# First maxima in ones and twos between the quarters of a feature product, and the last group's query blocks in the order second, third, fourth, first

## The chip, the cores and the metric

The kernel runs on one core of a Trainium2 chip. The metric is the device time of one execution in microseconds (us), the median of several runs. TensorE (PE) multiplies matrices into eight PSUM banks, VectorE (DVE) and ScalarE (ACT) work on PSUM and SBUF, GpSimd (POOL) on SBUF alone. SyncE (SP), ScalarE and GpSimd issue DMA transfers. The engines run on their own and wait for each other's semaphores.

## The reference

The input x is 2 x 2048 x 512. One transformer layer is computed in float32: causal attention with grouped keys, a layer norm, a soft mixture of experts, and a second layer norm. The change touches the attention alone:

```python
q = (x @ Wq).reshape(b, n, NUM_KV_GROUPS, GROUP_SIZE, HEAD_DIM)   # 4 groups of 4 heads, 32 wide
k = (x @ Wk).reshape(b, n, NUM_KV_GROUPS, HEAD_DIM)
v = (x @ Wv).reshape(b, n, NUM_KV_GROUPS, HEAD_DIM)
scores = jnp.einsum('bqgsd,bkgd->bgsqk', q, k) * scale
scores = jnp.where(causal, -jnp.inf, scores)
attn = jax.nn.softmax(scores, axis=-1)
ctx = jnp.einsum('bgsqk,bkgd->bqgsd', attn, v)
...
x = _layernorm(x + (ctx.reshape(b, n, D_OUT) @ Wo + bo), axis=-1)
```

## The kernel before

Five stages run one after the other, each ended by a barrier of all engines: `projections` (to 191.6 us), `attention` (to 1167.9 us), `post`, `slots` and `combine`.

**projections** works through eight blocks of 512 tokens (`NBLK`). For a block, TensorE transposes the input into the four banks of `ps_t`, and makes six features (`m` 0 to 3 queries of a group, 4 keys, `VT` = 5 values) into the four banks of `ps_f`. A feature is a sum over four quarters `c` of the 512 inputs, and each quarter takes three products (`three_passes`, L73 to L75), since every operand is split into a high and a low half. ScalarE reads a finished feature as its high half (`features_hi`, L320), VectorE makes the low half (`features_lo`, L356), and SyncE's `store` writes both to DRAM. SyncE's `first_loads` brings the first group's operands back into SBUF.

The softmax needs the largest score of each row ahead of the scores. One **unit** `u` is one product of 128 queries of a head with up to 512 keys; its rows' maxima are read by VectorE (`maximum`): by `tensor_reduce` where all keys are allowed, and by a masked form where the unit touches the diagonal. A unit's number of columns is 128, 256, 384 or 512. `MAXU` lists the units by query block. Those of the first two query blocks (`AHEAD` = 2), 48 units, are done inside projections, when `ps_t` has no more inputs to transpose: `units_behind(blk, m)` spreads them over ten places, each behind a whole feature, four or five at a place. Unit `u` takes bank `u % 4` of `ps_t` and waits until unit `u - 4` is read. VectorE takes a place's units right behind that feature's low half. After a query block's last unit, `maximum_rows` folds the maxima into rows (`s_max`), and SyncE copies each block's rows into `q` with four small transfers, at the very end of its work (L190).

**attention** has eight groups (`ITERS`: two batches, four key groups), each with four query blocks of 512 (`QB`). A query block `qb` has 4 * qb + 4 steps of 128 keys, so the first is short (4 steps) and the fourth long (16). A step has four **scores** (one per head, L1060), four exponentials on ScalarE (L1142) and a **context** product (L1078). The last four steps of a block lie on the diagonal: they are narrower (512, 384, 256, 128 columns), and GpSimd's `select` (L961) clears the upper triangle ahead of the context product. The sums of a row's exponentials are made partly on GpSimd, by `add` of whole steps (L981) and by transfers that add one step onto another (`move`, L994), partly on TensorE (`late_sums` L1089 for steps left over, `block_sums` L1098 for GpSimd's sum). VectorE turns them (`flip`, `inverse`), GpSimd multiplies (`normalise`, L1003), SyncE stores. The short block has no adds. A block's scores wait for its row transfers (`s_row`). A block's queries are loaded over those of the group before (`queries`, L889), as soon as the scores that read them are done.

The order of all this is written ahead by `plan()`: a greedy planner with modelled times chooses TensorE's next piece among scores, maxima (up to 80 units ahead of the scores, `M_LEAD`) and packed products. Every engine's program follows the list `order()`. `BLOCKS` gives the order of the query blocks: in each group 0, 1, 2, 3.

## Time and profile before

| | us |
|---|---|
| median of 3 runs (2526.11 to 2528.24) | 2528.2 |
| the profiled execution | 2528.26 |
| its span, first to last instruction | 2526.5 |
| attention's first product | 191.6 |
| last group's first score | 1033.9 |
| last exponential of attention | 1147.9 |
| post begins | 1167.9 |

The page gives for the span of 2526.5 us: TensorE busy 2413.8 us (96%), VectorE 1737.0, ScalarE 1426.1, GpSimd 1610.2. Busy times are averages over stages with different bounds; what counts at a place is which wait ends last there. All times below are us from the span's start.

### The profile page before, as it was taken

To read this page: it belongs to the slowest core of one execution; us is meant where nothing else is said; L and a number is where in the kernel's file an instruction comes from. 1 tells how busy PE (TensorE), PEld (TensorE's weight loads), DVE (VectorE), ACT (ScalarE), POOL (GpSimd) and SP (SyncE) were. 2 spreads that over 40 slices of the span, in tenths; PEclk is the share of its full clock that TensorE was granted. 3 is DMA by queue.
4 is the path that set the end of the run, shared out by engine and by line. 5 is a ranking of instruction groups with operands and counts; after the bars stand their busy time and mean duration, and the time that the engine had idled before them with its cause. 6 is when DMAs were issued, how large, how long until landed. Compare 5 with 4: busy or idle time off the path is not lost. (4 is left out here: it accounts for less than half of the span.)

```text
span 2526.5 us, 38828 instructions
## 1 busy us (share of the span) xinstructions
PE 2413.8 (96%) x12834; PEld 1726.7 (68%) x12834; DVE 1737.0 (69%) x3804; ACT 1426.1 (56%) x2761; POOL 1610.2 (64%) x1751
## 2 busy tenths in 40 slices
PE   8979999999999999996979999999999997999998
PEld 6865555555555555544767888887888885788886
DVE  3358778888888888833876655666656564877776
ACT  3215556666666666663865555666656554454553
POOL 4404577777877767776957667675576765555554
PEclk9999899999999999998989999999999998999999
DMA  7853655574656566555964545466445457674553
GB/s 248 270 169 84 132 124 125 115 151 113 145 112 145 118 144 123 116 107 157 355 202 138 166 137 159 145 217 186 152 141 160 132 164 245 189 226 131 148 151 102
DMA packets 249177, 400.87 MB, mean 159 GB/s; under 512 B 57712, under 2 KB 112016, under 8 KB 237584
## 3 DMA queue, kind: packets, MB, share of 16 engines
q1 hardware_dynamic: 196000, 283.48, 36.8%
q0 software_dynamic: 52480, 114.37, 20.5%
q8 instruction: 102, 1.67, 0.3%
q14 instruction: 99, 0.81, 0.1%
q10 hardware_dynamic: 496, 0.54, 0.1%
HBM read 180.63 MB, written 112.22 MB: 116 GB/s over the span
## 5 line engine op out<-in xcount | busy, mean ns | idle before, releaser
L1142 ACT ACTIVATE p_probs<-p_ps_s 128x512 f32<-128x512 f32 (+3 forms) x1280 | 591.1, 541 | 327.0 <-PE p_ps_s L1060 310.1
L1727 POOL DMA_DIRECT2D p_eT<-p_ex x1024 | 538.4, 535 | 272.9 <-DVE p_ex L1993 220.4
L1169 DVE TENSOR_REDUCE p_parts<-p_ps_m 128x1 f32<-128x512 f32 x752 | 459.1, 681 | 82.9 <-PE p_ps_m L1045 74.6
L1060 PE MATMUL p_ps_s<-q,k_e 98*128 98x512 f32 (+3 forms) x1280 | 468.4, 387 | 3.5 <-ACT p_probs L1142 3.1
L1045 PE MATMUL p_ps_m<-k_m,q 96*128 96x512 f32 (+2 forms) x1232 | 434.6, 387 | 11.9 <-PEq L2268 10.2
L981 POOL TENSOR_TENSOR p_added<-p_added,p_probs 128x2048 f32<-128x2048 f32 x88 | 419.4, 4769 | 34.5 <-ACT p_probs L1142 17.0
L1060 PEld LDWEIGHTS p_ps_s<-q,k_e 98*128 98x128 f32 x1280 | 241.8, 191 | 183.6 <-ACT p_probs L1142 76.3
L1078 PE MATMUL p_ps_c<-p_probs,v_e 128*32 128x512 f32 (+3 forms) x2560 | 285.3, 547 | 10.0 <-POOL p_probs L961 10.0
L1045 PEld LDWEIGHTS p_ps_m<-k_m,q 96*128 96x128 f32 x1232 | 235.4, 194 | 86.4 <-DVE p_parts L1173 20.2
L2127 POOL TENSOR_TENSOR p_acc<-p_acc,logit 128x512 f32<-128x512 f32 x112 | 162.5, 1451 | 153.6 <-ACT logit L2180 150.1
L1173 DVE CUSTOM_DVE_ANT_0 p_masked<-p_ps_m,p_mask 128x128 f32<-128x128 f32 (+1 forms) x480 | 203.9, 485 | 25.7 <-PE p_ps_m L1045 25.6
L73 PE MATMUL p_ps_l<-kept_hi,w_o_lo 128*128 128x512 f32 x512 | 208.0, 406 | 7.1 <-DVE w_o_lo L1940 6.4
L73 PE MATMUL p_ps_s<-xl_hi,w_o_hi 128*128 128x512 f32 x512 | 205.6, 402 | 8.8 <-DVE w_o_hi L1987 8.8
L74 PE MATMUL p_ps_s<-xl_lo,w_o_hi 128*128 128x512 f32 x512 | 204.7, 400 | 0.0
L75 PE MATMUL p_ps_s<-xl_hi,w_o_hi 128*128 128x512 f32 x512 | 204.7, 400 | 0.0
L1847 ACT ACTIVATE logit<-p_ps_l,kept_inv 128x512 f32<-128x512 f32 x128 | 87.8, 687 | 203.0 <-PE p_ps_l L75 203.0
L75 PE MATMUL p_ps_l<-kept_hi,w_o_lo 128*128 128x512 f32 x512 | 201.7, 394 | 0.0
L74 PE MATMUL p_ps_l<-kept_xT,w_o_lo 128*128 128x512 f32 x512 | 201.0, 393 | 0.0
L2180 ACT ACTIVATE logit<-logit 128x512 f32<-128x512 f32 x128 | 80.7, 631 | 150.4 <-DVE logit L2213 150.3
L1078 PEld LDWEIGHTS p_ps_c<-p_probs,v_e 128*32 128x32 f32 x2560 | 65.3, 110 | 126.1 <-issue 63.8
L1956 DVE TENSOR_REDUCE p_col<-logit 128x1 f32<-128x512 f32 x128 | 87.5, 684 | 85.3 <-ACT logit L1847 85.3
L1998 DVE TENSOR_TENSOR p_siT_lo<-p_ps_e,p_siT_hi 128x512 fp32r<-128x512 f32 x32 | 22.1, 692 | 159.3 <-ACT p_siT_hi L1882 159.3
(204 smaller groups left out, 4979.4 us busy)
## 6 DMA issues: line engine op xcount, KB each, us to landing
p_probs<-p_probs POOLq DMA_DIRECT2D x56, 1024.0 KB, 7.9
logits_t<-logit SPq DMA_DIRECT2D x32, 1024.0 KB, 5.0
p_eT<-p_ex POOLq DMA_DIRECT2D x1024, 32.0 KB, 2.1
logit<-logits_t SPq DMA_DIRECT2D x128, 256.0 KB, 3.5
q<-q_t SPq DMA_DIRECT2D x96, 256.0 KB, 4.8
c_first<-L_ffn_W_dram SPq DMA_DIRECT2D x64, 256.0 KB, 5.6
p_probs<-p_probs POOLq DMA_DIRECT2D x16, 768.0 KB, 7.5
p_x<-L_attn_x_dram SPq DMA_DIRECT2D x32, 256.0 KB, 4.7
```

Of the source, the lines that this page charges most:

```text
L73: pe.matmul(out, w_hi, m_hi, start=start, stop=False)
L74: pe.matmul(out, w_hi, m_lo, start=False, stop=False)
L75: return pe.matmul(out, w_lo, m_hi, start=False, stop=stop)
L981: pool.tensor_tensor(a[:, :, :], first[:, :, :], probs[s % RING][:, :, :], ALU.add).then_inc(s_add, 1)
L1045: pe.matmul(ps_m[:, bank("maximum", u), 0:w], q[0:QROWS, qb, h, bass.ts(t, P)], k_m[:, c * BLK:c * BLK + w], start=True, stop=True).then_i ...
L1060: pe.matmul(ps_s[:, u % ST_BANKS, q0:BLK], k_e[:, bass.ts(kt, P)], q[:, qb, h, q0:BLK], start=True, stop=True).then_inc(s_score, 1)
L1078: mm = pe.matmul(ps_c[part, 0, q0:BLK], v_e[:, kt, :], probs[s % RING][:, h, q0:BLK], start=s == FIRST[n], stop=last)
L1142: act.activation(probs[s % RING][:, h, q0:BLK], ps_s[:, u % ST_BANKS, q0:BLK], ACT.Exp).then_inc(s_exp, 1)
L1169: dve.tensor_reduce(to, bank, AX.X, ALU.max).then_inc(s_taken, 1)
L1173: dve.tensor_tensor_reduce(masked[u % 3][:, 0:w], bank, mask[:, BLK - w:], 1.0, -3.0e38, ALU.add, ALU.max, to).then_inc(s_taken, 1)
L1727: pool.dma_start(eT[r][p * QD:(p + 1) * QD, i, :, :], ex[i * QD:(i + 1) * QD, 2 * r:2 * r + 2, bass.ts(p, P)]).then_inc(s_eT[r], 16)
L2127: pool.tensor_tensor(a[:, :], a[:, :], lg[n % U][:, :], ALU.add).then_inc(s_acc, 1)
```

## The change

It has four parts. (1) The first 48 units get 36 places: behind each quarter `c` of the products of features 2 to 5 of block 6 and 0 to 4 of block 7, one unit or two. VectorE takes a feature's units ahead of that feature's low half. The value feature of the last block has no units. (2) `send_rows(0)` moves into SyncE's store of the last block, ahead of feature 2; `send_rows(1)` goes to ScalarE, behind its last copy. (3) In the last group, the query blocks come in the order 1, 2, 3, 0; `PREV` and `NEXT` name a block's counterpart in the neighbouring groups, and waits on key and value parts stand at every first use of a part. (4) VectorE waits for its mask at the first masked unit instead of at attention's start.

```diff
-        places = [(NBLK - 2, m) for m in range(2, VT + 1)] + [(NBLK - 1, m) for m in range(VT + 1)]
+        places = [(NBLK - 2, m, c) for m in range(2, VT + 1) for c in range(DC)] + [(NBLK - 1, m, c) for m in range(VT) for c in range(DC)]
-        def units_behind(blk, m):
+        def units_behind(blk, m, c):
...
+        def send_rows(eng, n):
+            eng.wait_ge(s_max, n + 1)
+            for a in range(4):
+                to = first[0][QROWS:MROWS, n, :, :].rearrange("o h (t a j) -> o h t a j", t=4, a=4)[:, :, :, a, :]
+                eng.dma_start(to.bitcast(F32), rows[n][a * 32:(a + 1) * 32, :]).then_inc(s_row[n], 16)
@@ sync: store
                 for m in range(NF):
+                    if blk == NBLK - 1 and m == 2:
+                        send_rows(sp, 0)
@@ sync: end
-            for n in range(AHEAD):
-                sp.wait_ge(s_max, n + 1)
...
@@ tensor: features
                         last = three_passes(pe, ps_f[:, bank(blk, m), :], w_hi[:, c, w], w_lo[:, c, w],
                                             xT_hi[j][:, c, :], xT_lo[j][:, c, :], c == 0, c == DC - 1)
+                        for u in units_behind(blk, m, c) if c < DC - 1 else []:
+                            unit(u)
                     last.then_inc(s_f, 1)
-                    for u in units_behind(blk, m):
+                    for u in units_behind(blk, m, DC - 1):
                         unit(u)
@@ scalar: end
+            for n in range(1, AHEAD):
+                send_rows(act, n)
@@ vector: features_lo
                 for m in ms:
+                    for c in range(DC):
+                        for u in units_behind(blk, m, c):
+                            maximum(u)
                     dve.wait_ge(s_fhi, blk * NF + (m + 1))
...
-                    for u in units_behind(blk, m):
-                        maximum(u)
@@
-BLOCKS = [(n // QB, n % QB) for n in range(NBK)]
+BLOCKS = [(it, qb) for it in range(ITERS) for qb in (range(QB) if it + 1 < ITERS else (1, 2, 3, 0))]
+SAME = {(it, qb): n for n, (it, qb) in enumerate(BLOCKS)}
+PREV = [SAME.get((it - 1, qb)) for it, qb in BLOCKS]
+NEXT = [SAME.get((it + 1, qb)) for it, qb in BLOCKS]
@@ attention, sync: queries
-                sp.wait_ge(s_score, 4 * END[n - QB])
+                sp.wait_ge(s_score, 4 * END[PREV[n]])
@@ attention, tensor: unit, scores, context
-                    if c == qb:
-                        pe.wait_ge(s_km[c], 48 * it)
+                    pe.wait_ge(s_km[c], 48 * it)
...
+                if it > 0 and kt % 4 == 0 and h == 0:
+                    pe.wait_ge(s_ke[kt // 4], 48 * it)
...
+                if it > 0 and kt % 4 == 0:
+                    pe.wait_ge(s_v[kt // 4], 16 * it)
@@ attention, vector
+                    if u == FIRST_MASKED:
+                        dve.wait_ge(s_mask, 1)
...
-            dve.wait_ge(s_mask, 1)
```

TensorE in projections, block 6, feature 2 (`p_ps_f` is the feature's bank, `p_ps_t<-k_m,q` a unit). Before:

```order
L73 MATMUL p_ps_f<-p_xT_hi,p_w_hi 128x512
L74 MATMUL p_ps_f<-p_xT_lo,p_w_hi 128x512
L75 MATMUL p_ps_f<-p_xT_hi,p_w_lo 128x512
L282 MATMUL p_ps_t<-k_m,q 128x128 x4
L73 MATMUL p_ps_f<-p_xT_hi,p_w_hi 128x512
```

and after, the feature's first two quarters and what follows the third:

```order
L73 MATMUL p_ps_f<-p_xT_hi,p_w_hi 128x512
L74 MATMUL p_ps_f<-p_xT_lo,p_w_hi 128x512
L75 MATMUL p_ps_f<-p_xT_hi,p_w_lo 128x512
L288 MATMUL p_ps_t<-k_m,q 128x128
L73 MATMUL p_ps_f<-p_xT_hi,p_w_hi 128x512
L74 MATMUL p_ps_f<-p_xT_lo,p_w_hi 128x512
L75 MATMUL p_ps_f<-p_xT_hi,p_w_lo 128x512
L288 MATMUL p_ps_t<-k_m,q 128x128
...
L288 MATMUL p_ps_t<-k_m,q 128x128 x2
```

The four units that stood behind the feature's last quarter now stand one, one, two behind its first three quarters.

SyncE at the end of projections: the last block's stores, the values' store and the row transfers. Before:

```order
L155 DMA q_t<-p_f_lo 128x512
L155 DMA k_t<-p_f_hi 128x512
L155 DMA k_t<-p_f_lo 128x512
L157 DMA v<-p_v 128x4x128
L190 DMA q<-first_rows 2x16x32 x8
```

and after, from the store of feature 1:

```order
L164 DMA q_t<-p_f_lo 128x512
L145 DMA q<-first_rows 2x16x32 x4
L164 DMA q_t<-p_f_hi 128x512
...
L164 DMA k_t<-p_f_lo 128x512
L166 DMA v<-p_v 128x4x128
```

Four row transfers now stand ahead of six stores, and the values' store is SyncE's last; the other four follow ScalarE's last copy (L333).

GpSimd at attention's end (`p_added` an add, `p_out` the product of normalise). Before:

```order
L981 TENSOR_TENSOR p_added<-p_added,p_probs 128x2048
L961 AFFINE_SELECT p_probs<-p_probs 128x4x128 x3
L981 TENSOR_TENSOR p_added<-p_added,p_probs 128x2048 x2
L1003 TENSOR_TENSOR p_out<-p_raw,p_inv 128x512
```

and after:

```order
L995 TENSOR_TENSOR p_added<-p_added,p_probs 128x2048
L975 AFFINE_SELECT p_probs<-p_probs 128x4x128 x3
L995 TENSOR_TENSOR p_added<-p_added,p_probs 128x2048
L975 AFFINE_SELECT p_probs<-p_probs 128x4x128 x2
L995 TENSOR_TENSOR p_added<-p_added,p_probs 128x2048
L975 AFFINE_SELECT p_probs<-p_probs 128x4x128 x2
L1017 TENSOR_TENSOR p_out<-p_raw,p_inv 128x512 x2
```

Two of the short block's selects stand ahead of the long block's last add, two behind it, and two products end the stage instead of one. On TensorE, the long block's first score is score 1217 of 1280 before and 1201 after, and the short block's 16 scores are the last. In groups one to seven no instruction of attention changes its place.

## Rows read from the trace of the kernel before

**Rows 1.** The page, part 2: granted TensorE clock in 40 slices of 63.2 us, tenths.

```profile
PEclk9999899999999999998989999999999998999999
```

**Rows 2.** Busy time of stretches: stretch, length, each engine's us, clock, DMA share, GB/s.

```profile
134.90:181.40 46.50, 39.43 (x178) 30.76 (x176) 30.58 (x93) 6.93 (x12) 0.00 (x0) 1.00 0.60 178
181.40:191.60 10.20, 0.03 (x1) 0.01 (x1) 2.81 (x12) 0.00 (x0) 0.02 (x1) 0.64 0.12 31
191.60:198.10 6.50, 6.48 (x16) 5.31 (x17) 4.98 (x8) 3.40 (x7) 1.54 (x5) 0.51 0.48 163
```

**Rows 3.** Waits from 140 to 192 us: waiter and releaser, us in total, times, longest.

```profile
PE p_ps_t L282 <- DVE p_parts L380: 4.7, 4, 1.3
...
PE p_ps_t L282 <- DVE p_parts L374: 2.2, 2, 1.2
```

**Rows 4.** TensorE's timeline: start, length, instruction, count, and the idle time before it.

```profile
179.49 1.50 PE L282 MATMUL p_ps_t<-k_m,q 96*128 96x384 f32 x5
...
191.62 0.77 PE L1045 MATMUL p_ps_m<-k_m,q 96*128 96x512 f32 x1 [10.19 <-PEq L2268]
```

**Rows 5.** VectorE's timeline: five unmasked maxima, and the last copy of the values.

```profile
156.68 3.07 DVE L374 TENSOR_REDUCE p_parts<-p_ps_t 128x1 f32<-128x512 f32 x5
...
183.67 0.65 DVE L366 COPY p_v<-p_ps_f 128x512 f32<-128x512 f32 x1
```

**Rows 6.** SyncE's queue: the values of block 6, the last key store, the row transfers.

```profile
165.03 0.37 SPq L157 DMA_DIRECT2D v<-p_v  x1
...
177.08 0.64 SPq L155 DMA_DIRECT2D k_t<-p_f_lo  x1
...
184.76 5.37 SPq L190 DMA_DIRECT2D q<-first_rows  x8
```

**Rows 7.** ScalarE's timeline: the last copy of projections, the last exponentials of attention.

```profile
179.69 0.60 ACT L327 ACTIVATE p_vT<-p_ps_f 128x512 f32<-128x512 f32 x1 [4.35 <-PE p_ps_f L75]
...
1146.63 1.25 ACT L1142 ACTIVATE p_probs<-p_ps_s 128x256 f32<-128x256 f32 x5 [1.51 <-PE p_ps_s L1060]
```

**Rows 8.** Busy time of three stretches of the last group.

```profile
1033.70:1094.20 60.50, 60.50 (x440) 34.49 (x441) 49.79 (x124) 39.11 (x85) 41.20 (x25) 1.00 0.40 88
1094.20:1147.90 53.70, 48.35 (x259) 18.75 (x257) 6.62 (x22) 36.82 (x82) 44.48 (x20) 0.94 0.58 118
1147.90:1167.90 20.00, 7.25 (x64) 2.33 (x64) 2.60 (x5) 0.60 (x1) 13.72 (x7) 0.73 0.04 14
```

**Rows 9.** TensorE's timeline: the long block's first scores, its product of sums.

```profile
1102.26 0.97 PE L1060 MATMUL p_ps_s<-q,k_e 98*128 98x512 f32 x3 [0.21 <-DMA q<-p_rows]
...
1160.65 1.94 PE L1098 MATMUL p_ps_m<-p_added,p_ones 128*32 128x512 f32 x8 [5.07 <-POOL p_added L981]
```

**Rows 10.** GpSimd's timeline at attention's end.

```profile
1149.27 2.10 POOL L961 TENSOR_SCALAR_AFFINE_SELECT p_probs<-p_probs 128x512 f32<-128x512 f32 x3
1151.05 9.46 POOL L981 TENSOR_TENSOR p_added<-p_added,p_probs 128x2048 f32<-128x2048 f32 x2
1164.76 1.26 POOL L1003 TENSOR_TENSOR p_out<-p_raw,p_inv 128x512 f32<-128x512 f32 x1 [4.26 <-issue]
```

**Rows 11.** TensorE's timeline, the short block: narrow scores, two contexts, late sums.

```profile
1044.12 0.33 PE L1060 MATMUL p_ps_s<-q,k_e 98*128 98x128 f32 x2
...
1047.36 1.28 PE L1078 MATMUL p_ps_c<-p_probs,v_e 128*32 128x384 f32 x16
...
1050.54 2.36 PE L1089 MATMUL p_ps_m<-p_probs,p_ones 128*32 128x512 f32 x32
```

**Rows 12.** The query loads of line 889: time from issue to landing.

```profile
DMA to landing us min/median/max: 3.8/4.8/8.1
```

**Rows 13.** Stretches of the first group, columns as before, and TensorE's timeline there.

```profile
266.00:270.00 4.00, 2.48 (x13) 0.59 (x16) 1.05 (x8) 0.28 (x1) 3.42 (x5) 0.52 0.00 0
282.00:286.00 4.00, 3.96 (x17) 2.50 (x13) 3.74 (x14) 0.92 (x2) 3.08 (x1) 0.84 0.00 0
...
267.66 3.21 PE L1078 MATMUL p_ps_c<-p_probs,v_e 128*32 128x512 f32 x16 [1.52 <-POOL p_probs L961]
```

More of the change, by code:

```diff
@@ L185, in _ @@
                 store(blk)
-            for n in range(AHEAD):
-                sp.wait_ge(s_max, n + 1)
-                for a in range(4):
-                    to = first[0][QROWS:MROWS, n, :, :].rearrange("o h (t a j) -> o h t a j", t=4, a=4)[:, :, :, a, :]
-                    sp.dma_start(to.bitcast(F32), rows[n][a * 32:(a + 1) * 32, :]).then_inc(s_row[n], 16)
         @block.gpsimd
@@ L406, in _ @@
                 features_lo(blk, range(2, NF))
-                for u in units_behind(blk, VT):
-                    maximum(u)
+                for c in range(DC):
+                    for u in units_behind(blk, VT, c):
+                        maximum(u)
             values(NBLK - 1)
@@ L434 @@
 U0 = M_END[AHEAD - 1]
+FIRST_MASKED = min(u for u in range(U0, NU) if MAXU[u][1] == BLOCKS[MAXU[u][0]][1])
 ADDED = [[], [0, 1, 3], [0, 1, 2, 3, 5, 6, 7], [0, 2, 4, 6, 7, 9, 11]]
@@ L538, in maximum_ready @@
         n = MAXU[u][0]
[L539 removed]
+        if PREV[n] is not None and 4 * END[PREV[n]] - 1 not in self.scored:
             return INF
[L541 removed]
+        return max(self.bank_free(), self.scored[4 * END[PREV[n]] - 1] + 6000 if PREV[n] is not None else 0)
     def ring_free(self, s):
@@ L672, in scores @@
             self.jobs.append((lambda: self.move_ready(s), "move", s))
-        if s == END[n] - 1 and n + QB < NBK:
-            self.moves.append((self.scored[u], "queries", n + QB))
+        if s == END[n] - 1 and NEXT[n] is not None:
+            self.moves.append((self.scored[u], "queries", NEXT[n]))
         if qb == QB - 1 and it + 1 < ITERS and s - FIRST[n] in (3, 7, 11, 15):
```

10 lines of the change are left out of this document (2 added, 8 removed).

## Prediction

> **What bounds the kernel now.** I read the granted clock by slices first, then the busy time of stretches, then the timelines of the two places that the change touches. TensorE's clock is at nine tenths or more in 36 of 40 slices [rows 1]; slice 5 (253 to 316 us) and slice 19 (1137 to 1200 us) hold two of the four dips, and the second lies at attention's end. The change touches the last 47 us of the first stage with the hand-over to attention, and the last 134 us of attention. All else, post, slots and combine (from 1167.9 us), keeps its instructions, so it should move as a block.
>
> First place. From 134.9 to 181.4 us TensorE is busy 39.4 of 46.5 us while VectorE works 30.6 us [rows 2]. The waits are TensorE's for VectorE: 6.9 us in six waits of up to 1.3 us, each at the fifth first maximum behind a feature, whose bank of ps_t is not yet read [rows 3]. Then TensorE stands still for 10.2 us: the last five maxima start at 179.49, and attention's first product at 191.62 [rows 4]. What fills the gap: VectorE reads maxima until 183.7 and copies the values at 183.67 to 184.32 [rows 5]; SyncE then issues the values' store and eight row transfers in 5.37 us, until 190.13 [rows 6]; the barrier takes 1.5 us more. The stage ends with SyncE's queue.
>
> Second place. Until 1094.2 us TensorE is busy all 60.5 of 60.5 us: TensorE bound. From there to 1147.9, with no maxima left, it is busy 48.4 of 53.7, and in the 20.0 us after the last exponential 7.3 [rows 8]. In those 20 us GpSimd sets the pace: three selects, two adds of together 9.46 us to 1160.5, then the block's product of sums, flip, inverse and the output's product at 1164.76 [rows 9, 10].
>
> **The change, part by part.**
>
> *Maxima one by one.* The same 48 units go behind 36 quarters, one or two each, instead of four or five behind ten features. Products added: none; removed: none. What goes is the 6.9 us. Is VectorE fast enough? A feature costs TensorE 12 products at 0.228 us (2.74 us) and 5.3 units at up to 0.235 us (1.25), 3.98 us. VectorE needs 5.3 x 0.61 us (five in 3.07 [rows 5]) plus the low half at 0.61, 3.88 us. That is nearly even where units are 512 wide (u 10 to 31), looser elsewhere. With four banks between them I keep 0.7 us of waits. Ends: 0, and 6.9 if the wait returns at other places. On the other side the last five units (1.1 us) now lie ahead of the value feature, no longer behind it. The value feature so ends at 179.5 - 6.9 + 0.7 + 1.1 = 174.4.
>
> *What follows it.* After the value feature no maxima are queued on VectorE, only the values: ScalarE's copy 0.2 us behind the feature, 0.60 us long [rows 7], the transposes, VectorE's copy 0.65: done 2.3 us after the feature, at 176.7; before it was 4.8 us.
>
> *Row transfers.* Eight at 0.67 us each [rows 6] were SyncE's last work. Now four stand in SyncE's store of the last block, four on ScalarE behind its last copy. ScalarE: 174.4 + 0.8 + 4 x 0.67 = 177.9. It delays nothing there, since ScalarE has no more work in the stage; its price on ScalarE's queue isn't in the trace, ends 1.2 to 4 us in all. SyncE's queue has to be followed too, for all is queued behind it: from the store of block six's values at 165.03 to the last key store's end, 177.72, it issues 21 transfers in 12.7 us [rows 6]. That start depends on VectorE's copy of those values, which comes 3.5 us sooner (the three waits ahead of it, 3.5, less four more units, 0.9, and a copy no longer queued behind four maxima, about 0.9). So 161.5 + 12.7 + 2.7 = 176.9, then the values' store at 177.3. ScalarE ends last at 177.9, SyncE 0.6 us before. Barrier 1.4: attention starts at 179.3 instead of 191.6. **Gain 12.3 us**, ends 8 and 14.5.
>
> *The mask wait* moves from VectorE's start of attention to its first masked unit. VectorE's first unit was released within 0.2 us of it: nothing.
>
> *The clock at the hand-over.* It fell 3 us into the idle time and came back 6.4 us after attention began; the stretch 191.6 to 198.1 ran at 0.51 [rows 2]. The idle time shrinks from 10.2 to some 4 us, and a wait of only 1.52 us, near 266 us, lies in a stretch at 0.52 [rows 13]. So I expect it to fall still, and come back a little sooner: 0.5 us, ends 0 and 3.
>
> *Order of the last group.* Up to the group's start nothing moves. The short block (16 scores, 4 contexts, 4 late sums) goes from first to last. While TensorE is the bound, its work is time: scores at 0.11 to 0.24 us each (two narrow ones in 0.33), 2.6 us; contexts 2.7 (the middle two 1.28); late sums 2.36 [rows 11]; 7.7 us. Also the third block's last, narrow scores stood alone before, after the last maximum, and waited for ScalarE: about 1.8 us, which go since maxima now stand between them. The long block so starts 9.5 us sooner than 1102.26 [rows 9] counted from the group's start. Ends 7 and 11.
>
> Does something hold it back? The long block's queries are now wanted twenty scores sooner. Their load starts with the group, has three transfers and takes 3.8 to 8.1 us each, median 4.8 [rows 12]; TensorE reaches the first unit that needs them some 6 us after the group starts. Wait 0.2 us, ends 0 and 3.3. The long block's row transfers get as much work ahead of its first score as before: no wait.
>
> *The tail.* T is the last exponential of the long block; before, attention ended at T + 20.0. The long block's run (45.6 us) and GpSimd's work in it stay. Now: add done T + 1.4, three selects to T + 3.2, add to T + 7.8, the short block's first two selects (1.25) to T + 9.1, add to T + 13.7, two selects to T + 15.0 [rows 10]. Beside these, ScalarE's 16 exponentials end by T + 11 (the last five took 1.25 [rows 7]). Then on TensorE the block sums (1.0 at full clock, 1.94 before [rows 9]) to T + 15.3, contexts 0.9, late sums 2.4 [rows 11] to T + 19.0; flip, reciprocal, transpose 2.0; product 1.3; to the next stage 1.9: T + 24.3. That is 4.3 us longer, ends 0 and 8. **Gain 9.5 - 4.3 - 0.2 = 5.0 us.**
>
> **Sum.** 12.3 + 0.5 + 5.0 = 17.8 us. The profiled execution took 2528.26 us (span 2526.5 and 1.8 around it), the median is 2528.2. So 2528.3 - 17.8 = **2510.4 us**. With the ends of the large terms halved against each other, 2506 to 2515.
>
> A rule speaks against the one-by-one form. In the trace the 6.9 us of short waits left the clock at 1.00 until 181 us, but the wait of 1.52 us before 267.66 us lies in a stretch at 0.52, and the clock was not back until the stretch 282 to 286 us [rows 2, 13]. The Trainium skill, page "TensorE: Matmul & The Clock Gate", section "A second HAM failure mode: psum-queue depth-cycling", says that small pauses between groups of products that cycle through PSUM banks make the clock swing between its levels. By that rule the 36 places could do this, and the sum would lose 8 us and more (rivals three and four); by the rows alone it loses nothing.
>
> **The rivals.**
>
> *One, VectorE sets the pace* in the first stage. 3.88 against 3.98 us per feature is close, and the low half now waits behind its feature's units. If 4 us of waits come back, the value feature ends at 178 and attention starts at 183: 2514 us. For it: the even pace. Against it: VectorE's whole work there, 30.6 us, is 9 less than TensorE's [rows 2].
>
> *Two, the tail eats the gain.* The short block's contexts and sums stand in TensorE's queue behind the long block's product of sums, which waits for GpSimd's last add, and GpSimd takes two selects ahead of that add. If the tail is T + 28 and the long block gains 7: minus 1 instead of plus 5, 2516 us.
>
> *Three, a clock spell.* One at half clock as after 266 us: the shifted start meets a pause at another moment. Some sixteen us at half clock [rows 13] cost up to 8 us: 2518. The same spell could vanish instead, which would give 2503.
>
> *Four, slower than before.* Each of the 36 places makes TensorE wait for VectorE's read, and the clock stays at 1.2 GHz for the stretch of 39 us of work. Price 39 us at most, 2549 us. It decides from the point where more than about 18 us are lost, 0.5 us a place or 18 us of work at half clock in that stretch; slower by over 0.2% from 23 us. Against it: the clock's row stays at 1.00 through waits of 1.3 us there.
>
> **How the numbers follow.** Forecast 0.72; one 0.12; two 0.08; three 0.05; four 0.03. A measurement tells about 0.2% (5 us) from no change. The first four cases are faster by more, less a 0.02 for several misses at once; that 0.02 is within; four is slower: faster 0.95, same 0.02, slower 0.03. The range from 2504 to 2518 takes in the forecast's ends, case one, two and most of three.
>
> **What the profile after would show.** Attention's first product at 179.3 (177 to 183), TensorE's waits for maxima in the first stage under 1.5 us, ScalarE's row transfers ending last before the barrier. The long block's first score near 1080.5, its last exponential near 1126, post's start near 1150. The forecast is wrong if the waits in the first stage stay above 3 us, if SyncE ends over 1 us after ScalarE, if the long block's first score is less than 7 us closer to the group's start, or if the tail behind its last exponential is over 28 us.

## The result and the profile after

The changed kernel took 2503.6 us, the median of four runs (2497.7 to 2505.7), against 2527.15 before (2525.9 to 2528.2). The ratio is 0.9903, with an interval from 0.9888 to 0.9919: 24 us, or 1%, faster. The forecast of 2510.4 was wrong: the gain is larger than the 17.8 us forecast, and the median lies 0.4 us under the range. The profiled execution is the fastest of the four, 2497.7 (span 2496.0). Below, lines of this trace stand beside those of before, and a second trace of the same kernel (`e5_after`) says which of the differences belong to the kernel.

The clock in 40 slices, page of the changed kernel, part 2. Slice 5 (250 to 312 us) is at nine tenths or more; before it was at eight [rows 1].

```profile
PEclk9999999999999999999989999999999997999999
```

**The first stage.** Busy time of stretches: stretch, length, then TensorE, its weight loads, VectorE, ScalarE and GpSimd in us, granted clock, DMA share, GB/s. First the changed kernel, from block 5's copy of the value feature to block 7's, then the hand-over, attention's first 4 us, and 163 us from attention's start.

```profile
127.01:171.74 44.73, 44.70 (x216) 37.00 (x214) 35.45 (x106) 9.25 (x16) 0.00 (x0) 1.00 0.65 186
171.74:177.00 5.26, 0.63 (x5) 0.45 (x5) 0.69 (x1) 0.60 (x1) 0.04 (x1) 0.73 0.94 336
177.00:181.00 4.00, 4.00 (x10) 3.17 (x11) 2.71 (x4) 2.00 (x4) 0.88 (x4) 0.50 0.79 258
177.00:340.00 163.00, 157.98 (x983) 90.25 (x987) 133.01 (x346) 91.54 (x197) 95.72 (x54) 0.95 0.51 114
```

The kernel before, first and last of these stretches:

```profile
127.47:179.69 52.22, 45.15 (x213) 36.23 (x212) 31.09 (x91) 9.24 (x17) 0.00 (x0) 1.00 0.61 185
191.60:354.60 163.00, 159.16 (x957) 92.30 (x957) 128.79 (x337) 88.21 (x190) 93.64 (x52) 0.89 0.50 109
```

TensorE's idle time in the stretch fell from 7.07 us to 0.03, and the stretch from 52.22 to 44.73: 7.5 us. The waits have turned round. In the changed kernel, from 140 to 192 us, this is who waited for whom (us in total, times, longest):

```profile
DVE p_x L389 <- PE p_ps_t L288: 2.5, 10, 0.5
```

No line with TensorE waiting for a maximum is left [rows 3]; VectorE now waits for the units. The timeline of the hand-over, changed kernel (start, length, engine, instruction, idle time before it and its releaser; SPq and ACTq are the DMA issues of SyncE and ScalarE):

```profile
171.74 0.60 ACT L333 ACTIVATE p_vT<-p_ps_f 128x512 f32<-128x512 f32 x1 [2.61 <-PE p_ps_f L75]
171.75 3.74 ACTq L145 DMA_DIRECT2D q<-first_rows  x4
...
172.68 0.64 SPq L164 DMA_DIRECT2D k_t<-p_f_lo  x1
173.15 0.69 DVE L375 COPY p_v<-p_ps_f 128x512 f32<-128x512 f32 x1 [1.62 <-PE p_ps_f L295]
173.87 0.37 SPq L166 DMA_DIRECT2D v<-p_v  x1
...
177.00 0.77 PE L1058 MATMUL p_ps_m<-k_m,q 96*128 96x512 f32 x1 [3.88 <-PEq L2282]
```

ScalarE's queue ends last, at 175.49, and attention starts at 177.00, 14.6 us sooner than at 191.62 [rows 4]. Of these, 0.45 us are a delay that the trace before had earlier: block 5's copy already stood at 127.47 there and at 127.01 here. The change's own share is 14.2.

**The last group**, changed kernel: the group's start to the long block's first score; from there to that block's last exponential; from there to post.

```profile
1011.88:1072.95 61.07, 60.02 (x401) 32.99 (x399) 49.58 (x135) 38.29 (x83) 47.13 (x23) 1.00 0.43 92
1073.00:1116.80 43.80, 39.62 (x217) 15.28 (x218) 5.04 (x16) 31.11 (x65) 34.54 (x16) 0.95 0.63 132
1116.80:1139.20 22.40, 16.04 (x144) 7.43 (x143) 4.29 (x8) 7.09 (x18) 17.01 (x12) 0.80 0.07 24
```

The first two of the kernel before; its third is the last of [rows 8], 20.00 us long:

```profile
1033.90:1102.20 68.30, 67.92 (x482) 37.96 (x481) 53.61 (x140) 44.56 (x100) 48.35 (x29) 1.00 0.36 79
1102.20:1147.90 45.70, 40.72 (x216) 15.07 (x216) 2.60 (x5) 31.17 (x66) 37.12 (x16) 0.93 0.67 138
```

The group with its tail took 127.3 us instead of 134.0. Its three parts changed by -7.2, -1.9 and +2.4 us. The end of the tail, changed kernel, GpSimd's last add and what TensorE does behind it (the long block's product of sums, then the short block's late sums):

```profile
1125.35 4.76 POOL L995 TENSOR_TENSOR p_added<-p_added,p_probs 128x2048 f32<-128x2048 f32 x1
...
1130.26 1.07 PE L1111 MATMUL p_ps_m<-p_added,p_ones 128*32 128x512 f32 x8 [1.05 <-POOL p_added L995]
...
1131.76 2.36 PE L1102 MATMUL p_ps_m<-p_probs,p_ones 128*32 128x512 f32 x32
```

**Where the 30.5 us between the two traces went.** I took the start of the same score in both traces. Attention's first: 14.6. The 201st score, which is 40 scores into the second group: 19.4. The last group's first: 22.1 (1011.88 against 1033.95). Post: 28.7. End: 30.5. In `e5_after` the same points give 14.7, 15.1, 17.3, 23.5 and 24.4. So the 4.4 us by which the first trace is ahead at the 201st score aren't the kernel's. Between that score and the last group's first, where no instruction moved, both traces gain 2.2 to 2.6 us, and most of the others gain as much: units alone 1.9, the first stage 2.0, the order 1.6, the row transfers 2.2, VectorE's order 2.5. Only `e7_filled`, in which the stretch has the same instructions, gains 0.4. What differs is how long TensorE waits there for a `select` of GpSimd: 2.2 us in the kernel before, 1.9 in `e7_filled`, 0 to 1.0 in the ten others that have the same instructions there. So the trace before is at the long end of a spread, and these 2 us aren't shown to be the change's. The longest of its waits is this one:

```profile
837.45 0.85 PE L1078 MATMUL p_ps_c<-p_probs,v_e 128*32 128x384 f32 x8 [1.10 <-POOL p_probs L961]
```

### The profile page after: what moved, and what is told of

Same layout as the page of the kernel before. It is cut to its first block and busy times, and to the rows that moved or that the text cites. A ratio compares the mean times of both kernels' runs of the same rounds, so it can differ in the third digit from the quotient of the medians.

```text
span 2496.0 us, 38932 instructions
## 1 busy us (share of the span) xinstructions
PE 2400.8 (96%) x12834; PEld 1717.9 (69%) x12834; DVE 1735.2 (70%) x3804; ACT 1426.8 (57%) x2761; POOL 1610.6 (65%) x1751
## 5 line engine op out<-in xcount | busy, mean ns | idle before, releaser
L1058 PE MATMUL p_ps_m<-k_m,q 96*128 96x512 f32 (+3 forms) x1232 | 431.1, 384 | 6.6 <-PEq L2282 3.9
L1058 PEld LDWEIGHTS p_ps_m<-k_m,q 96*128 96x128 f32 x1232 | 231.6, 191 | 84.9 <-DVE p_parts L1188 22.3
L73 PE MATMUL p_ps_s<-xl_hi,w_o_hi 128*128 128x512 f32 x512 | 204.3, 399 | 13.6 <-DVE w_o_hi L2001 13.6
L2012 DVE TENSOR_TENSOR p_siT_lo<-p_ps_e,p_siT_hi 128x512 fp32r<-128x512 f32 x32 | 22.1, 691 | 158.8 <-ACT p_siT_hi L1896 158.8
```

What stands on the lines that cost most here:

```text
L73: pe.matmul(out, w_hi, m_hi, start=start, stop=False)
L1058: pe.matmul(ps_m[:, bank("maximum", u), 0:w], q[0:QROWS, qb, h, bass.ts(t, P)], k_m[:, c * BLK:c * BLK + w], start=True, stop=True).then_i ...
```

## The experiments

My theory: the gain is a sum of its places (start of attention about 14 us, last group about 7), and what is left is half clock that differs from run to run. The rival: the one-by-one form changes the clock of the first groups and so brings more than its place. In all of these kernels the mask wait, and TensorE's waits for key and value parts, stand where the change put them.

| kernel | median, us | gain by the ratio, us (interval) |
|---|---|---|
| e1_units | 2515.4 | 9.9 (6.3 to 13.4) |
| e2_stage_one | 2507.8 | 19.0 (15.9 to 22.0) |
| e3_order | 2518.0 | 8.1 (4.8 to 11.1) |
| e4_rows | 2522.0 | 5.1 (2.5 to 7.6) |
| e5_after | 2503.9 | 23.8 (20.5 to 26.8) |
| e6_vector_first | 2518.4 | 8.6 (5.6 to 11.6) |
| e7_filled | 2504.1 | 22.2 (19.0 to 25.5) |
| e8_order_2310 | 2529.0 | -1.5 (-4.0 to 1.0) |
| e9_less_add | 2505.9 | 21.2 (17.9 to 24.8) |
| e10_rows_split | 2500.4 | 26.5 (23.0 to 30.1) |
| e11_order_2130 | 2511.7 | 14.7 (11.4 to 17.7) |
| e12_both | 2504.0 | 22.0 (18.7 to 25.5) |

A gain is the ratio's distance from one, and its ends', times the median of the kernel before that was measured beside it, 2526.7 to 2527.3.

### Units alone

```diff
@@ on the changed kernel
-            for n in range(1, AHEAD):
-                send_rows(act, n)
@@ sync, end
+            for n in range(AHEAD):
+                send_rows(sp, n)
-... else (1, 2, 3, 0))]
+... else (0, 1, 2, 3))]
```

`send_rows(0)` ahead of feature 2 in SyncE's store goes as well.

> The first maxima one by one alone; the eight row transfers stay at SyncE's end and the last group keeps the order 0, 1, 2, 3 (VectorE's mask wait stands as in the changed kernel). Theory one, the gain is the sum of its places: the value feature ends near 172 us (7.5 us sooner than before), the values' store is issued at 174, the eight row transfers take 5.4 us behind it, attention's first product stands at 180 to 182, and the time is 2516 to 2518 (10 to 11 us less than before). Theory two, the one-by-one form above all takes half-clock spells away from the first groups: attention's first product near 181 as well, but the time is 2509 or less, and the mean granted clock is 0.976 or higher against 0.972 before.

The value feature's copy starts at 171.80. SyncE's queue is what the theory says, and the first product follows at 181.19:

```profile
173.92 0.37 SPq L164 DMA_DIRECT2D v<-p_v  x1
174.34 5.38 SPq L145 DMA_DIRECT2D q<-first_rows  x8
```

The time, 2515.4, is 0.6 us under the first theory's range. The mean clock of its runs was 0.970 to 0.974, with 0.971 to 0.975 before: the rival's higher clock isn't there.

### The whole first stage

Units and row transfers as in the changed kernel, the last group in its old order.

```diff
-... else (1, 2, 3, 0))]
+... else (0, 1, 2, 3))]
```

> The first maxima one by one and the row transfers moved to SyncE's last store and to ScalarE; the last group keeps the order 0, 1, 2, 3. Theory one: attention's first product at 177, 14.2 us sooner than before, and the time 2512 to 2514; the mean clock of the runs differs from run to run in the same way as before. Theory two (spells go away with this form): 2506 or less, mean clock 0.976 or more in every run.

The first product stands at 176.66, as expected. The time, 2507.8, lies between what the two theories gave. The first theory's 2512 to 2514 mean a gain of 13 to 15 us, and the interval, 15.9 to 22.0, lies above that: its place was right, its time missed by 4 us. In its trace the start of attention gives 15.0 us, the 201st score 15.5, the last group's first 17.5. So nothing of note is added up to the 201st score (0.5 us), and the 2 us behind it are those of the trace before. This trace is of the longest of its six executions (2509.9), and what made the median 2 us shorter stays open. The clock of its runs, 0.973 to 0.977, is not always at 0.976: theory two falls in the form in which it was put. That some of the time gained comes through the clock is neither shown nor excluded at this size.

### The order alone

The changed kernel with units and row transfers as before.

```diff
-        places = [(NBLK - 2, m, c) for m in range(2, VT + 1) for c in range(DC)] + ...
+        places = [(NBLK - 2, m, DC - 1) for m in range(2, VT + 1)] + [(NBLK - 1, m, DC - 1) for m in range(VT + 1)]
```

VectorE takes them behind the low half again, and the eight transfers are at SyncE's end.

> The order 1, 2, 3, 0 in the last group alone. Theory one: the long block's first score comes 7.2 us sooner counted from the group's first score, its run is 1.6 us shorter, the tail behind its last exponential is 2.2 us longer; from the group's first score to post 127.3 us instead of 134.0, and the time 2520 to 2521 (6.6 us less). Theory two (much of the gain is clock): 2523 or more, the group's 127.3 us was a run with little half clock there.

From the group's first score to post it took 125.9 us, 8.0 less than before; by the places, that is the order's gain in this trace. The time, 2518.0, is 2 us under the first theory's 2520 to 2521, and its gain of 8.1 us has an interval (4.8 to 11.1) that holds the 5.0 forecast too. Its three stretches, columns as above:

```profile
1031.00:1092.10 61.10, 59.98 (x401) 33.01 (x399) 49.65 (x135) 38.24 (x83) 47.23 (x23) 1.00 0.43 92
1092.10:1134.40 42.30, 38.07 (x217) 14.61 (x218) 5.03 (x16) 30.95 (x65) 34.51 (x16) 1.00 0.66 137
1134.40:1157.00 22.60, 16.24 (x144) 7.56 (x143) 4.29 (x8) 7.17 (x20) 17.20 (x13) 0.80 0.06 24
```

The first and the third agree with the changed kernel's within 0.2 us. The second is 1.5 us shorter, at a clock of 1.00 instead of 0.95: the same work, 38.07 us busy instead of 39.62. The remaining 1.9 us against the kernel before (43.80 to 45.70) are its half clock too (0.93) and 0.8 us of waits. It is no accident of two traces: the long block's run took 45.2 to 46.1 us in the five traces with the old order (6.2 to 7.8 us at half clock) and 42.3 to 44.0 in the seven with the order 1, 2, 3, 0 (0.2 to 4.2 us at half clock). Why the clock falls less there stays open.

### The row transfers alone

Units behind whole features and order as before, only the `send_rows` calls moved.

> Only the row transfers moved (four in SyncE's last store, four behind ScalarE's last copy), maxima four or five behind a feature as before, order as before. Theory one: the second block's rows are ready near 183.7 us, ScalarE issues its four until 186.5, SyncE's store of the values is issued at 184.5: attention's first product at 188, 3 to 4 us sooner, and the time 2523 to 2524. Rival: the four transfers ahead of SyncE's last stores delay the values' store as much as they save behind it, and the time is that of before.

The first product stands at 187.77, 3.1 us sooner once the 0.7 us are taken off by which the whole trace is ahead at block 5. ScalarE's four transfers start when the second block's rows are ready and end the stage; SyncE's store comes without delay:

```profile
183.07 3.21 ACTq L145 DMA_DIRECT2D q<-first_rows  x4
183.63 0.38 SPq L166 DMA_DIRECT2D v<-p_v  x1
```

The median, 2522.0, is 1 to 2 us under the expectation, with an interval that holds it (2.5 to 7.6). The rival falls. By first products, units alone give 10.0 us, transfers alone 3.1, together 14.2: with units one by one the transfers save 1.1 us more. There ScalarE's four begin with the value feature's copy (171.75 and 171.74); here they wait for the second block's rows until 4.1 us behind it (183.07 and 178.97).

### The changed kernel again

> The changed kernel once more, for the spread of its own runs. Theory one (the parts add up, the rest is half-clock spells that differ from run to run): attention's first product at 177 within 0.6 us, from the last group's first score to post 126 to 128 us, both as in the first look; the time somewhere from 2497 to 2506, median 2500, with the spells of the first group at other places than in the first look. Theory two (the two parts get in each other's way): 2503 to 2505 in nearly all runs and the first look was the exception.

First product 176.91, group to post 127.7 us, median 2503.9 with runs from 2502.2 to 2505.5. The places are as in the first trace, so the parts hold; but the times are those of theory two: 2497.7 was the exception. That the parts get in each other's way isn't shown by it: the gains of the whole first stage (19.0) and of the order (8.1) sum to 27.1 us against 23.8, which their intervals of 3 us each way allow. The 4.4 us up to the 201st score are most of the 6.1 us between the two profiled executions. The stretch of 163 us from attention's start, of `e5_after`, beside 0.95 in the first trace and 0.89 before:

```profile
177.00:340.00 163.00, 157.28 (x959) 91.31 (x960) 129.21 (x339) 88.16 (x190) 93.59 (x52) 0.91 0.48 110
```

From attention's first score to its 201st, the traces of all kernels of this document have 17 to 37 us at half clock: the changed kernel's first 17, the kernel before 36.5, `e5_after` 29. The same stretch took 168.8, 173.6 and 173.2 us in these three, and 171.7 to 177.7 in the others. The first two traces stand near the two ends of this spread.

### VectorE's order alone

TensorE keeps the ten places behind whole features. VectorE reads a place's units ahead of the feature's low half.

```diff
@@ vector: features_lo, as in the change
+                    for c in range(DC):
+                        for u in units_behind(blk, m, c):
+                            maximum(u)
                     dve.wait_ge(s_fhi, blk * NF + (m + 1))
...
-                    for u in units_behind(blk, m):
-                        maximum(u)
```

> Of part one only VectorE's order: TensorE keeps the ten places of four or five units behind whole features, and VectorE reads a place's units ahead of the feature's low half instead of behind it. Row transfers and last group as before. Theory one (what TensorE waited for was VectorE's late start on a place, 1.4 us behind the feature; a wait costs its idle time and 0.28 us more): the fifth unit waits some 0.2 us instead of up to 1.3, together with the 0.28 some 2.7 us are left of 8.6, the value feature ends near 174 us, attention's first product stands at 185 to 186, and the time is 2521. Theory two (the interleaving on TensorE is what counts, since the reads take 0.61 us each and TensorE makes a unit in 0.23): the waits stay above 5 us and the time is above 2525.

The stretch from block 5's to block 7's value feature, and a place of five units with the product behind it:

```profile
126.93:172.72 45.79, 45.14 (x213) 36.25 (x212) 31.11 (x91) 9.24 (x17) 0.00 (x0) 1.00 0.62 186
```

```profile
152.54 1.68 PE L288 MATMUL p_ps_t<-k_m,q 96*128 96x512 f32 x5
154.06 0.40 PE L73 MATMUL p_ps_f<-p_xT_hi,p_w_hi 128*128 128x512 f32 x1
```

Theory one holds: 6.4 of the 7.5 us come from VectorE's order alone, and interleaving on TensorE adds 1.1, although four more units (0.9 us) then lie ahead of the value feature. The first product stands at 184.65, a little sooner than expected, and the time is 2518.4, 2.6 less than expected. The written waits are down to 0.4 us in two places. The row of five also shows what a column hides: five units of 512 columns need 1.17 us at 0.235 each, the next product starts 1.52 us behind the first, and yet no idle time is written. The fifth unit starts 0.48 us behind the fourth, 0.25 late; the fourth's record is 0.40 us long and covers most of that. Another 0.10 us are behind the fifth. So a pause as short as this doesn't show in the idle column.

The kernel before, the place at 155.25, with such a pause beside its written wait:

```profile
155.25 1.09 PE L282 MATMUL p_ps_t<-k_m,q 96*128 96x512 f32 x4
157.42 0.50 PE L282 MATMUL p_ps_t<-k_m,q 96*128 96x512 f32 x1 [1.08 <-DVE p_parts L374]
157.76 0.40 PE L73 MATMUL p_ps_f<-p_xT_hi,p_w_hi 128*128 128x512 f32 x1
```

The fifth unit would stand at 156.19 and stands at 157.42: 1.23 us late, where the column writes 1.08. The product behind it starts 0.34 us after it, where the step is 0.24 in the changed kernel (166.47 and 166.71):

```profile
166.47 0.40 PE L288 MATMUL p_ps_t<-k_m,q 96*128 96x512 f32 x1
166.71 0.40 PE L73 MATMUL p_ps_f<-p_xT_hi,p_w_hi 128*128 128x512 f32 x1
```

Summed from start to start over the whole stretch, the kernel before took 14.44 us for 35 steps from unit to unit, `e6_vector_first` 8.02 for the same 35. In the changed kernel all steps behind a unit take 8.53 us for 48 units, in the kernel before 16.72 for 44.

### The hand-over filled

```diff
             values(NBLK - 1)
+            pe.wait_ge(s_taken, M_END[AHEAD - 1])
+            for i in range(14):
+                pe.matmul(ps_t[:, i % DC, :], w_hi[:, 0, 0:P], xT_hi[(NBLK - 1) % 2][:, 0, :], start=True, stop=True)
```

> The changed kernel with 14 products more on TensorE, whose results nobody reads, in the idle time of the hand-over, behind the last transposes (173 to 176.3 us). Theory one (the half clock at attention's start comes from the idle hand-over): no half clock at 174 to 181, attention's first four us run at full clock and the time is 2 us less than the changed kernel's of the same call; the spells further on in the first group come from that group's own waits and stay. Theory two (the hand-over also sets off the spells behind it): the first group's spells go as well, 6 us and more less. Theory three: the products delay the barrier and nothing is gained.

Three stretches: the hand-over with attention's first 4 us, the first spell at half clock behind it, and attention's first 163 us (the first group and 20 us of the second).

```profile
174.00:181.00 7.00, 5.99 (x27) 4.28 (x25) 3.17 (x6) 2.92 (x6) 1.56 (x5) 1.00 0.75 258
...
209.10:222.70 13.60, 13.60 (x68) 7.75 (x72) 6.49 (x15) 1.30 (x4) 8.61 (x4) 0.50 0.51 103
...
177.00:340.00 163.00, 157.75 (x958) 90.39 (x958) 128.06 (x338) 87.69 (x190) 93.60 (x52) 0.91 0.49 110
```

The half clock at the start is gone (1.00, against 0.50 in the changed kernel). The seventeenth score came 1.1 and 1.8 us sooner than in the two traces of the changed kernel. But then a spell of 13.6 us came, where those had 6.8 and 3.4, and over the 163 us the clock is 0.91, as in `e5_after`. The time is 2504.1, the same. No theory stood as put: the first is right on the cause of the half clock at the start, but its 2 us were given back behind it. The total of half clock in this stretch may be set by its own work; one trace with a full hand-over doesn't show it, and what would remove it wasn't found.

### Third block first

```diff
-... else (1, 2, 3, 0))]
+... else (2, 3, 1, 0))]
```

> The changed kernel with the last group's order 2, 3, 1, 0 in place of 1, 2, 3, 0. Theory one (the long block's tail on GpSimd should lie beside work for TensorE): with 32 and 16 scores behind the long block, GpSimd's last adds are done long before TensorE's scores end, the idle time of TensorE in the group falls from about 6 us, and the group takes 3 us less: 3 us less than the changed kernel of the same call. Rival: the long block's scores wait for its query load, since it is wanted earlier still, or the exponentials of narrow scores set the pace at the end; same time or up to 4 us more.

It cost 25 us against the changed kernel, and neither theory had that. Of the last group, three stretches in which the long block's maxima are made:

```profile
1051.00:1061.50 10.50, 9.44 (x46) 5.09 (x44) 10.23 (x18) 3.35 (x11) 9.85 (x8) 0.99 0.43 75
1061.50:1068.30 6.80, 6.80 (x48) 3.29 (x48) 3.11 (x17) 0.60 (x1) 6.63 (x2) 0.52 0.00 0
...
1072.00:1080.00 8.00, 7.25 (x13) 3.73 (x14) 7.89 (x20) 0.00 (x0) 0.00 (x0) 0.50 0.01 2
```

In the first, VectorE is busy 10.23 of 10.5 us: it sets the pace, since 75 maxima stand within 40 scores (in the changed kernel about one to a score). TensorE waits between units for their banks; its clock falls at 1061.2 us, returns at 1068.0, and is at half again from 1071.4 to 1088.5. Of the 154 us that the group takes with its tail, 44.7 are at half clock (the 47.7 of the next expectation counts a spell whole that began before the group), against 12.8 in the changed kernel: up to 16 us of the loss. The Trainium skill, page "TensorE: Matmul & The Clock Gate", section "A second HAM failure mode: psum-queue depth-cycling", describes this pattern: small pauses between groups of products that cycle through banks make the clock swing. The trace agrees here in that the clock swung behind such pauses. The first stage of the kernel before doesn't agree: 7.07 us of waits for banks in 52.22 left the clock at 1.00. Beside the cluster, the group's first score waited 2.77 us for its block's row transfers, which neither the changed kernel nor the next order has.

### Third, second, fourth, first

```diff
-... else (1, 2, 3, 0))]
+... else (2, 1, 3, 0))]
```

> The changed kernel with the last group's order 2, 1, 3, 0. The order 2, 3, 1, 0 cost 26 us, with 75 maxima within 40 scores ahead of the long block's (VectorE busy 28.9 of 33 us there) and 47.7 us of half clock in the group. Here the maxima stand one to a score, as in the order 1, 2, 3, 0. Theory one (the cluster of maxima was what cost): within 2 us of the changed kernel, 2502 to 2506, and 10 to 17 us of half clock in the group. Rival (what costs is that the third block comes first, its queries' load and the thin stretch of maxima ahead of it): 2512 or more.

2511.7, between the two again: 8 us more than the changed kernel instead of 25. So theory one fell by its number, and by its half clock, which is 22.3 us in the group instead of 10 to 17. About 17 of the 25 us go with what sets the two orders apart, the second block behind the long one and with it the cluster and the wait of 2.77 us; that the cluster alone does it isn't shown. 8 us stay with the third block coming first. With the third block first, its maxima may start only when the same block of the group before is scored, and the stretch before that is thin:

```profile
940.00:980.00 40.00, 39.61 (x259) 19.51 (x257) 22.01 (x62) 24.39 (x52) 33.57 (x15) 0.91 0.54 110
```

VectorE works 22.0 of 40 us there, against 33.0 in the changed kernel, and TensorE has 6.8 us at half clock. 21 fewer units are made by the group's first score. Beside `e5_after`, this trace has 4.5 us more from the 201st score to the group's first, of which the half clock can be 3.4, and 5.1 us more in the group, 132.7 instead of 127.7, which has the 21 units to make and 9.5 us more at half clock. (The trace is of the longest of its five executions; that is why the two are more than 8.)

### One add less in the tail

```diff
-ADDED = [[], [0, 1, 3], [0, 1, 2, 3, 5, 6, 7], [0, 2, 4, 6, 7, 9, 11]]
+ADDED = [[], [0, 1, 3], [0, 1, 2, 3, 5, 6, 7], [0, 2, 4, 6, 7, 9, 11], [0, 2, 4, 6, 7, 9]]
```

The fifth list serves the last group's long block only.

> The changed kernel, and in the last group's long block step 11 is not added by GpSimd: it goes to TensorE's late sums (four more products), so one add of 4.8 us less stands in the tail. Theory one (behind the long block's last exponential GpSimd still sets the pace): the last add ends 5 us sooner, TensorE's wait of 1.05 us for it goes, the short block's scores and exponentials set the end, and from the last exponential of the long block to post it takes 20.5 us instead of 22.5; the time is 2 us less than the changed kernel's (2503.9 in its last series), so 2502. Rival (TensorE at half clock sets the tail): its 16 us of work stay and the time is the same within 0.5.

The tail from the long block's last exponential became 24.95 us instead of 22.5. GpSimd's last add did end sooner (7.7 us behind that exponential instead of 13.4), so the theory was right on GpSimd and wrong on what sets the end. TensorE's timeline there:

```profile
1129.10 3.39 PE L1107 MATMUL p_ps_m<-p_probs,p_ones 128*32 128x512 f32 x40
1132.42 0.62 PE L1078 MATMUL p_ps_s<-q,k_e 98*128 98x256 f32 x3
...
1138.76 0.43 PE L1096 MATMUL p_ps_c<-p_probs,v_e 128*32 128x128 f32 x8 [1.21 <-POOL p_probs L980]
1139.01 3.77 PE L1107 MATMUL p_ps_m<-p_probs,p_ones 128*32 128x512 f32 x32
```

GpSimd's, beside it:

```profile
1136.86 1.26 POOL L1022 TENSOR_TENSOR p_out<-p_raw,p_inv 128x512 f32<-128x512 f32 x1 [2.07 <-issue]
1138.07 0.64 POOL L980 TENSOR_SCALAR_AFFINE_SELECT p_probs<-p_probs 128x512 f32<-128x512 f32 x1
```

Eight products of late sums more (40 instead of 32; the expectation had counted four) stand ahead of the short block's next scores, which come 1.0 us later behind the long block's last exponential (1132.42, against 1130.40 in `e5_after`, whose exponential ended 1.0 us sooner). The short block's last context waits 1.21 us for its `select`, which now stands in GpSimd's queue behind the long block's output product. And the last 32 late sums take 3.77 us, since the clock fell at 1139.7, where they took 2.36 in the changed kernel. So the path to the end is TensorE's, as the rival said, but with a wait for GpSimd in it, and it is 2.5 us longer instead of the same.

### One row transfer on SyncE

```diff
+                        if blk == NBLK - 1 and m == NF - 1 and half == 1:
+                            send_rows(sp, 1, (3,))
                         sp.wait_ge(ready, blk * NF + (m + 1))
@@ scalar: end
-                send_rows(act, n)
+                send_rows(act, n, range(3))
```

> The changed kernel, and one of the second block's four row transfers is sent by SyncE ahead of the last key store instead of by ScalarE. ScalarE's four took 3.74 us and ended at 175.49, SyncE ended at 174.24. Theory one (ScalarE's queue ends the stage): it ends 0.9 us sooner, SyncE 0.1 later, attention's first product stands at 176.0 instead of 176.9, and the time is 0.9 less, 2503. Rival (something else holds the barrier): the first product stays at 176.9.

```profile
171.54 2.70 ACTq L145 DMA_DIRECT2D q<-first_rows  x3
...
172.73 0.63 SPq L145 DMA_DIRECT2D q<-first_rows  x1
...
174.04 0.55 SPq L168 DMA_DIRECT2D v<-p_v  x1
...
175.73 0.76 PE L1060 MATMUL p_ps_m<-k_m,q 96*128 96x512 f32 x1 [2.83 <-PEq L2284]
```

From the value feature's copy to attention's first product it takes 4.20 us here and 4.09 in `e12_both`; in the six traces with interleaved units, four transfers on ScalarE and an empty hand-over 4.72 to 5.26, mean 4.88. So 0.7 to 0.8 us, near the theory's 0.9, and ScalarE's queue was the end of the stage. Here SyncE's is: its store ends at 174.59, ScalarE's transfers at 174.24. Its median of 2500.4 is the lowest of all, 3 us under the changed kernel's; more than 0.8 of these can't be put down to the edit, since its runs spread from 2496.0 to 2505.1.

### Both edits

> The edits of the last two together: one add less in the tail, one row transfer on SyncE. If both theories hold they add up to 2.9 us less than the changed kernel, 2501; if neither, 2504.

2504.0, the number named for the case that neither theory holds; but the places say that one does: the tail took 25.0 us again and the hand-over 4.09. The loss of the one edit and the gain of the other cancel within what can be told. The split transfers alone are the form to keep.

## Why the prediction was wrong, point by point

The forecast of 2510.4 us was 6.8 us too long. 1.1 us of that is the base: I took the sum off 2528.3, the profiled execution, while the kernel before has a median of 2527.2 in 47 runs (2521.7 to 2533.5). The other 5.8 are the gain, 23.6 us instead of 17.8: 1.9 in the first stage with the hand-over, 1.3 to 3.0 in the last group, and some 1 to 3 that no place accounts for. Those are no more than the spread of the runs: the changed kernel's two series of four runs have medians of 2503.6 and 2503.9, the second just 0.1 us under the range.

**Maxima one by one: the failed term.** The step that failed is "What goes is the 6.9 us", of which 0.7 were to stay. The mechanism was right: TensorE's waits for a bank went, and went whole. But a wait cost more than its idle column. The value feature was forecast at 174.4, 5.1 us sooner; it came 7.5 us sooner (7.9 by the traces, less the 0.45 of the trace before). The true loss of the kernel before is read from the steps from start to start. 35 steps from unit to unit took 14.44 us and would take 6.3 at the widths' own 0.11, 0.12, 0.18 and 0.235 us, so 8.1 us were lost; another 0.1 us was lost behind each of eight places. From these 8.9 us, 0.9 go for four more units ahead of the feature, and 0.5 for the feature products, whose steps are 0.004 us longer in the changed kernel. The term was 6.2 us net and measured 8.9.

**What follows the value feature: right, with some luck.** The forecast went from 174.4 to 179.3, 4.9 us; measured 4.7 to 5.3. ScalarE's queue ended last, as said. But its four transfers began with the copy, not behind it, and took 0.94 us each instead of 0.67. The two cancel.

**Mask wait: nothing**, as far as the traces show. VectorE read its first unit 0.95 us behind attention's first product before, and 0.80 after. The move wasn't undone by itself.

**Clock at the hand-over: right on what it does, small in worth.** It still fell, 1.1 us behind the last transposes, and came back 4.0 us into attention instead of 6.3. The experiment that kept it up gave its gain back inside the first group.

**The last group: the sum of 5.0 us was too small, with three wrong parts that partly cancel.**

- The long block's start came 7.2 us sooner, forecast 9.5, ends 7 to 11. The 7.7 us for the short block's work are confirmed (TensorE's busy time went from 67.92 to 60.02, 7.9 less). The 1.8 us for waits of the third block's narrow scores were never there: the stretch before has 0.4 us of idle time in all, and the new one 1.1.
- The long block's run was to stay, and became 1.7 to 3.3 us shorter, most of it clock. This term was put at nothing.
- The tail was to grow by 4.3 us and grew by 2.4. The last add ended 13.4 us behind the last exponential (13.7 forecast), and TensorE's product of sums followed 0.1 us behind it. With contexts and late sums it ended at 17.4, where the forecast had 19.0. The forecast let the product start 0.8 us later, behind two selects that it doesn't wait for, and allowed 0.8 us more from there on; 0.4 of that is a slip, since its own terms (1.0, 0.9 and 2.4) lead from the product's start at 14.3 to 18.6 and not to 19.0.

The query load was to cost 0.2 us and cost nothing that a trace shows: the 0.22 us ahead of the long block's first score are for its row transfers, and the kernel before has 0.21 there [rows 9].

**The rivals.** VectorE did not set the pace in the first stage: it was busy 35.45 us of 44.73. The tail did not eat the gain, but it moved from GpSimd to TensorE, as the experiment with one add less shows. Of rival three, the clock spell, the other side ("which would give 2503") came true in part and in another place: 0.2 to 4.2 us at half clock in the long block's run, instead of 6.2 to 7.8, in every trace with the new order. The first trace's 19 us less at half clock ahead of the 201st score were luck of that execution, and `e5_after` has only 7 less. That side was in the text and not in the bounds. The slower case: TensorE waited at none of the 36 places, and the clock was at 1.00 throughout. The rule that I weighed there has no ground in the first stage after the change, because no pauses are left, and the pauses before the change left the clock up; only the order 2, 3, 1, 0 bears it out. The row that I set against the form, the wait of 1.52 us ahead of 267.66 [rows 13], doesn't show a fall that a pause set off either: the clock fell at 266.2 us, as that wait began, and TensorE's rows show no idle time in the 8 us ahead of it.

## What to carry to other kernels

Cost a stall between short products by the steps from start to start, not by the idle column. Ask first whether the engine that reads the result can take its work sooner: here the order on VectorE brought 6.4 us and the finer interleaving 1.1. Before an order of blocks is changed, count how many maxima stand between how many scores: the order with 75 maxima within 40 scores cost up to 16 us by the clock, and TensorE's written waits for maxima in that group were 1.6 us. And before two traces are subtracted, take a second one of the same kernel: here the two differ by 4.4 us in one stretch.

## What the runs showed of the hardware

Short pauses between products left no idle time in the profile's column: five units of 512 columns took 1.52 us where their steps need 1.17, with one of them 0.25 us late. Four small row transfers on ScalarE were issued while its copy of 0.60 us ran, at 0.94 us each (3.74 us); on an idle ScalarE they took 0.80 each (3.21 in `e4_rows`), on SyncE 0.67 (5.38 for eight). A full clock kept up through the hand-over did not lower the half clock of the 163 us behind it: 0.91 with it, 0.91 and 0.95 in two traces without. Two traces of one kernel have 0.91 and 0.95 in that stretch, which is 4.4 us of time. And a stretch in which VectorE was busy 10.23 of 10.5 us was followed by two falls of TensorE's clock, though TensorE was itself busy 9.44; in the first stage before the change it was busy 45.15 of 52.22 and the clock stayed up.
